# Experts' products of a transformer block in plain fp32 instead of three fp32r products, with a longer pipeline

## What is computed

```python
# 1. adapter with weights made from the condition
x0 = x + relu(x @ w_down(cond)) @ w_up(cond)
# 2. attention, causal, 16 query heads and 4 key/value heads of 64, RoPE, a sink in the denominator
x2 = x0 + attention(rmsnorm(x0, w1)) @ proj_w + proj_b
# 3. mixture of 32 experts, 4 per token
h2 = rmsnorm(x2, ffn_norm_w)
topv, topi = top_k(h2 @ gate_w + gate_b, 4);  gw = softmax(topv)
for n in range(32):                       # W_up[n]: 256 x 512, W_down[n]: 256 x 256
    ug = h2 @ W_up[n];  u, g = ug[:, :256], ug[:, 256:]
    y2 += combine[:, n] * ((silu(g) * u) @ W_down[n])
out = x + x2 + y2
```

## Time and profile before

| | |
|---|---|
| median of 3 runs | 1193.15 us (1192.16 to 1199.51) |
| the profiled execution: span | 1193.3 us |
| TensorE (PE) busy | 988.5 us, 83% |
| DVE busy | 766.5 us, 64% |
| POOL busy | 711.0 us, 60% |
| ACT busy | 451.5 us, 38% |
| read from HBM, written to HBM | 140.37 MB, 90.05 MB |
| first up product of stage two (L984) | 645.78 us |
| first sum of the tail (L1620) | 1161.07 us |

### The profile page before, as it was taken

The page is one execution under the profiler, slowest core; times in us unless marked ns, Lnnn a source line. Parts: engine busy times, 40 slices in busy tenths (PEclk is TensorE's granted clock), DMA queues, the critical chain, the costliest instruction groups (busy, mean ns, idle before and its releaser), DMA issues.

```text
span 1193.3 us, 19476 instructions
## 1 busy us (share of the span) xinstructions
PE 988.5 (83%) x6158; PEld 782.7 (66%) x6158; DVE 766.5 (64%) x1702; ACT 451.5 (38%) x1120; POOL 711.0 (60%) x672
## 2 busy tenths in 40 slices
PE   3779799999999998998834888888888888888896
PEld 1557576776767676676723776767767766676675
DVE  3868487776867777784672555555556555555568
ACT  1133243434343353424412444443444444444441
POOL 3426346858586776767485666666666666666550
PEclk8879899999999999998966999999999999999998
DMA  6328976565657756557566755574555546553498
GB/s 177 83 65 272 315 257 197 199 187 198 182 166 238 205 192 202 172 178 209 195 211 212 248 200 202 177 256 158 197 197 192 193 169 231 182 186 129 110 365 315
DMA packets 110749, 239.22 MB, mean 200 GB/s; under 512 B 19171, under 2 KB 48248, under 8 KB 109915
## 3 DMA queue, kind: packets, MB, share of 16 engines
q1 hardware_dynamic: 84042, 192.03, 48.5%
q0 software_dynamic: 19552, 40.02, 10.8%
q10 hardware_dynamic: 7056, 5.91, 1.6%
HBM read 140.37 MB, written 90.05 MB: 193 GB/s over the span
## 4 chain that ended last, share of the span: by engine, by line
PE 56%; DVE 19%; issue 9%; another core or an unknown queue 5%; ACT 4%; POOL 4%; DMA 2%; SPq 0%; ACTq 0%; DVEq 0%; POOLq 0%
PE gbank L984 16%; PE gbank L853 10%; PE gbank L1004 7%; PE gbank L778 4%; DVE ring L1339 4%; PE scores L814 4%; POOL lists L655 3%; ACT in_part L1194 2%; DVE in_part L1572 2%; PE gbank L756 2%; PE scores L995 2%; PE scores L957 2%; PE gbank L827 2%; PE gbank L748 1%
## 5 line engine op out<-in xcount | busy, mean ns | idle before, releaser
L984 PE MATMUL gbank<-ring,in_part 128*128 x954 | 271.4, 421 | 56.4 <-DVE in_part L1572 41.7
L700 POOL DMA_INDIRECT pick_rows<-rows_out,pair_row x156 | 161.0, 1032 | 150.9 <-ACT rows_out L1210 109.1
L984 PEld LDWEIGHTS gbank<-ring,in_part 128*128 128x128 f32 x954 | 173.3, 194 | 97.4 <-issue 67.8
L693 POOL DMA_INDIRECT rows_in<-x_rows,token_row x156 | 152.1, 975 | 55.4 <-issue 40.4
L1572 DVE SCALAR_TENSOR_TENSOR in_part<-scores,norm_w,in_part 128x128 fp32r<-128x128 f32 x318 | 96.3, 345 | 136.7 <-ACT in_part L1194 114.8
L1004 PE MATMUL gbank<-ring,mid_part 128*128 x954 | 155.7, 300 | 12.8 <-DVE mid_part L1593 9.3
L662 POOL TENSOR_TENSOR ring<-ring 128x512 fp32r<-128x512 f32 x96 | 121.0, 1279 | 72.1 <-ACT ring L1149 71.5
L655 POOL DMA_INDIRECT lists<-entry,slot_i x128 | 124.9, 976 | 38.8 <-issue 34.0
L853 PE MATMUL gbank<-w_o,ring 128*128 128x256 f32 x512 | 128.9, 409 | 17.1 <-DVE ring L1322 12.8
L1004 PEld LDWEIGHTS gbank<-ring,mid_part 128*128 128x128 f32 x954 | 126.6, 193 | 20.0 <-issue 19.9
L1210 ACT ACTIVATE rows_out<-gbank,gates 128x256 f32<-128x256 f32 x156 | 74.6, 478 | 154.5 <-PE gbank L1004 97.5
(11 more groups left out here) (169 smaller groups left out, 1495.3 us busy)
## 6 DMA issues: line engine op xcount, KB each, us to landing
w_parts<-ring SPq DMA_DIRECT2D x192, 256.0 KB
ring<-w_parts SPq DMA_DIRECT2D x32, 1536.0 KB
ring<-in_W_up SPq DMA_DIRECT2D x64, 256.0 KB
q_r<-rot SPq DMA_DIRECT2D x32, 512.0 KB, 6.1
picks<-pick_rows SPq DMA_DIRECT2D x8, 2048.0 KB
lists<-in_fill_slots SPq DMA_DIRECT2D x36, 256.0 KB, 5.0
ring<-in_W_down SPq DMA_DIRECT2D x32, 256.0 KB
x_t<-in_x_t SPq DMA_DIRECT2D x8, 512.0 KB, 5.0
```

What stands on the lines that cost most here:

```text
L693: e.indirect_dma_start(out=rows_in[i % NG][:, :], out_offset=None, in_=x2_rows, in_offset=bass.IndirectOffsetOnAxis(ap=begun[:, i, 3:4].bi ...
L700: e.indirect_dma_start(out=pick_rows, out_offset=bass.IndirectOffsetOnAxis(ap=begun_row[:, i:i + 1] if i < AHEAD else pair_row[:, i:i + 1] ...
L984: ins = e.matmul(bank[:, :], in_parts[i % 2][x][:, c, :], ring[:, bass.ds(at + y * WE + c * 2 * DFF, 2 * DFF)], start=k == 0, stop=k == le ...
```

## The change

The experts' products are computed in plain fp32: per tile 2 matmuls of 512 columns up and 2 of 256 down, on weights loaded from W_up and W_down as they lie, with two DMAs per expert (512 and 256 KB) straight into the ring. All load_third, split and store_third steps are gone from the lists of SP, ACT and POOL, and what is left of SP's list is spaced anew. The ring has 8 slots of one copy each; its last six lie over buffers of stage one (y_t, tmp, rot, prob_t), so experts 0 and 1 are loaded after SP's steps, 2 to 7 once stage one has let go of these. The turned rows (in_t) are one copy, the first half written by ACT, the second by DVE; the turned mid (mid_t) is one copy by DVE.

TensorE's order per tile becomes turn_mid(i-2), turn_in(i+2) with the wait for the expert's weights between its two transposes, expert_up(i), expert_down(i-3). turn_in and up share four PSUM banks, turn_mid and down four others. There are 3 buffers of in_t and mid, 8 of gathered rows (NG), 6 of rows_out (NY), and the scatter goes from i-2 to i-4. NET becomes 161, NPICK 5. The plan divides by 8 with a shift.

```diff
-NET = PAIRS // P + E - 1
-RING = 3
-AHEAD = RING
+AHEAD = 3
+NET = PAIRS // P + E - 1 + (AHEAD - 1)
+RING = 8
+FRONTS, BACKS = 4, 4
+IN_BUFS, MID_BUFS = 3, 3
-NW, NU, NPAY, NG, NY, NC = 5, 3, 3, 6, 4, 4
+NPAY, NG, NY, NC = 3, 8, 6, 4
-NPICK = 6
+NPICK = 5
...
     "POOL": ("""
         up pair pair pair pair pair up
     """, """
-        split split pair pair split split pair pair split split pair route_put split split split
-        route_put up route_put split split split route_put
+        pair pair pair pair pair route_put route_put up route_put route_put
     """, """
-        split split split split split route_put split split route_put split route_put split split split
-        route_put split route_put route_put route_put route_put
+        route_put route_put route_put route_put route_put route_put route_put route_put
...
         def load_expert(n):
             r = n % RING
-            e.dma_start(ring[:, r * 2 * WE:(r + 1) * 2 * WE].bitcast(F32).rearrange("p (h n) -> p h n", h=2),
-                        w_parts[n].rearrange("h p n -> p h n")).then_inc(s_weight[r], 16)
+            slot = ring[:, r * WE:(r + 1) * WE]
+            e.dma_start(slot[:, 0:KC * 2 * DFF].rearrange("p (c n) -> p c n", c=KC),
+                        d["W_up"][n].rearrange("(c p) n -> p c n", p=P)).then_inc(s_weight[r], 16)
+            e.dma_start(slot[:, KC * 2 * DFF:WE].rearrange("p (c n) -> p c n", c=FC),
+                        d["W_down"][n].rearrange("(c p) n -> p c n", p=P)).then_inc(s_weight[r], 16)
...
-        for i in range(NET + 2):
+        for i in range(NET + 4):
             if i + NG - 1 < NET:
                 gather(i + NG - 1)
-            if i >= 2:
-                scatter(i - 2)
+            if i >= 4:
+                scatter(i - 4)
...
+        def turn_in(i, ready=None):
+            bank = front[i % FRONTS]
             w.wait_ge(s_rows_in[i % NG], 16 * (i // NG + 1))
-            if i >= 2:
-                w.wait_ge(s_in_lower, i - 1)
+            if i >= FRONTS:
+                w.wait_ge(s_mid, i - FRONTS + 1)
             for c in range(KC):
+                if c == 1 and ready is not None:
+                    e.wait_ge(s_wready, ready)
                 ins = e.transpose(bank[:, c * P:(c + 1) * P], rows_in[i % NG][:, c * P:(c + 1) * P], ident[:, :])
...
-            for k, (c, x, y) in enumerate(CHUNK_PRODUCTS):
-                ins = e.matmul(bank[:, :], in_parts[i % 2][x][:, c, :],
-                               ring[:, bass.ds(at + y * WE + c * 2 * DFF, 2 * DFF)],
-                               start=k == 0, stop=k == len(CHUNK_PRODUCTS) - 1)
+            for c in range(KC):
+                ins = e.matmul(front[i % FRONTS], in_t[i % IN_BUFS][:, c, :], ring[:, bass.ds(at + c * 2 * DFF, 2 * DFF)],
+                               start=c == 0, stop=c == KC - 1)
             ins.then_inc(s_ug, 1)
...
         def expert_down(i):
-            out, at = gbank[2 + i % 2][:, 0:D], slot_of[i][0]
+            out, at = back[i % BACKS][:, D:2 * D], slot_of[i][0]
             w.wait_ge(s_mid_parts, i + 1)
-            if i >= 2:
-                w.wait_ge(s_rows_out, i - 1)
-            for k, (c, x, y) in enumerate(CHUNK_PRODUCTS):
-                ins = e.matmul(out, mid_parts[i % 2][x][:, c, :],
-                               ring[:, bass.ds(at + y * WE + KC * 2 * DFF + c * D, D)],
-                               start=k == 0, stop=k == len(CHUNK_PRODUCTS) - 1)
+            for c in range(FC):
+
+                if c == 1 and i + 2 >= BACKS:
+                    w.wait_ge(s_rows_out, i + 2 - BACKS + 1)
+                ins = e.matmul(out, mid_t[i % 2][:, c, :], ring[:, bass.ds(at + KC * 2 * DFF + c * D, D)],
+                               start=c == 0, stop=c == FC - 1)
             ins.then_inc(s_used, 1)
...
-        for i in range(NET + 2):
+        for i in range(NET + 3):
+            if i == 5:
+                w.wait_ge(s_gates, 2)
+            if 2 <= i < NET + 2:
+                turn_mid(i - 2)
             if i < NET:
+                ready = slot(i)[1]
+                if 0 < i < NET - 2:
+                    turn_in(i + 2, ready)
+                else:
+                    e.wait_ge(s_wready, ready)
                 expert_up(i)
...
-        def split(q):
-            w.wait_ge(s_whole[q % NW], 16 * (q // NW + 1))
-            if q >= NU:
-                w.wait_ge(s_lower, q - NU + 1)
-                w.wait_ge(s_upper_out[q % NU], 16 * (q // NU))
-            e.activation(w_upper[q % NU], w_third[q % NW].bitcast(F32), ACT.Copy).then_inc(s_upper, 1)
...
         def expert_down(i):
 
-            w.wait_ge(s_used, i + 2)
             if i >= NY:
                 w.wait_ge(s_put[i % NY], 16 * (i // NY))
+            w.wait_ge(s_used, i + 2)
```

More of the change, by code:

```diff
@@ L124 @@
     """, """
[L125 to L128 removed]
+        store_x2 store_x2 store_x2 store_x2
     """),
@@ L414, in program @@
              "slot_i"))
[L415 to L416 removed]
+    (s_list_tile, s_expert, s_gates, s_token_row, s_ring_wait, s_plan, s_in_whole, s_mid, s_mid_parts, s_final) = (
+        sem(f"s_{n}") for n in ("list_tile", "expert", "gates", "token_row", "ring_wait", "plan", "in_whole", "mid",
                                 "mid_parts", "final"))
@@ L1220, in scalar_program @@
         w.wait_ge(s_begun, 16)
-        for i in range(NET + 2):
+        for i in range(NET + 3):
+            if 0 < i < NET - 2:
+                turn_in(i + 2)
             if i < NET:
                 expert_up(i)
-            if i >= 2:
-                expert_down(i - 2)
-            if i + 2 < NET:
-                turn_in(i + 2)
+            if i == 0:
+                turn_in(2)
+            if i >= 3:
+                expert_down(i - 3)
             if i % XSTEP == 0 and 2 <= i // XSTEP < 2 + NT // NX:
@@ L1535, in vector_program @@
         e.tensor_scalar(of_tile[:, 3, :], of_tile[:, 0, :], float(E - 1), None, ALU.min).then_inc(s_expert, 1)
-        assert RING == 3 and all(43 * k >> 7 == k // RING for k in range(E))
+        assert RING == 8
         w.wait_ge(s_plan_row, 1)
-        got = own.mark(e.tensor_scalar(plan_e[:, :], plan_row, 43.0, None, ALU.mult))
+        got = own.mark(e.tensor_copy(plan_e[:, :], plan_row))
         w.wait_ge(s_vector, got)
-        got = own.mark(e.tensor_scalar(plan_e[:, :], plan_e[:, :], 7, None, ALU.arith_shift_right))
+        got = own.mark(e.tensor_scalar(plan_e[:, :], plan_e[:, :], 3, None, ALU.arith_shift_right))
         w.wait_ge(s_vector, got)
@@ L1604, in vector_program @@
         for i in range(NET + 2):
+            if i == 1:
+                slots()
+            if i >= 2:
+                turn_mid(i - 2)
+            if 0 < i < NET - 2:
+                turn_in(i + 2)
             if i < NET:
                 expert_mid(i)
-            if 1 <= i <= NET:
-                turn_mid(i - 1)
-            if i == 1:
-                slots()
-            if i + 2 < NET:
-                turn_in(i + 2)
+            if i == 0:
+                turn_in(2)
             if i % XSTEP == 0 and 3 <= i // XSTEP < 3 + NT // NX:
```

204 lines of the change are left out of this document (64 added, 140 removed).

## The result

The kernel after takes 1228.44 us (median of 4 runs, 1225.15 to 1230.91) beside 1194.08 for the kernel before: ratio 1.028, interval 1.026 to 1.031. Forecast were 1170 us (1145 to 1216). It is slower where it was forecast faster.

The account below looks back on a forecast made before the run. TensorE was taken to bound stage one, and TensorE and POOL neck and neck, with stalls, stage two. 1193.3 - 12.5 (stage two) - 4 (stage one) - 8 (transition) = 1168.8, forecast as 1170 us, range 1145 to 1216.

Parts of the forecast that it names:

- Products, tiles and stalls in stage two: Stage two: 161 fp32 tiles of 3.02 us, stalls nearly gone, 502.7 us against 515.2, so -12.5 us.
- the 8 us for left-over stalls: Stage two: 0.05 us of stall per tile left, 8 us in all; bounds nothing and today's 0.65 per tile.
- two readings of the stall: Stage two: rows_out's four slots wait for the scatter of i-4, or TensorE's signal comes late while POOL issues indirect DMAs.
- Rival A: Stage two: late signals still stall the ring of dependences; 1265 us with all stalls kept, 1213 with half; chance 0.15.
- Weights and tail: Stage two and tail: expert weights loaded early cost nothing; one pick buffer less costs 0, at worst +4 us.
- Splits out of stage one: Stage one: removing POOL's splits, ACT's copies and their loads and stores gives -4 us, bounds +10 and -30.
- the transition: Between stages: the last 32 puts, without 7 splits between them, end 8 us earlier; bounds -10 and -3.
- my 12: Stage one and transition together: -4 us for the splits and -8 us for earlier last puts.
- rival C: Whole kernel: no stalls, freer DVE and half of stage one's 36 idle us gone, 1148 us; chance 0.11.
- Rival B: Stage one: late signals beside runs of eight puts, 4 to 5 us in six periods, +24 to +30; 0.22 with partial stalls.
- 103 us of stalls removed: Stage two of the kernel before: some 103 us of waits, 0.65 per tile, of which the change would leave 8.
- The rule that I weighed: Stage one: VectorE and GpSimd share ports, first starter keeps them; removing 121 us of splits would then give more than 4 us.

Follow-up runs that it names:

- before_four_3: Kernel before with a fourth fp32r product per chunk in the up product, in a held session: 1205.36 us, ratio 1.010 to the kernel before.
- before_pipe: Kernel before, its fp32r products and split weights kept, with after's stage-two pipeline (order, banks, buffers, scatter i-4), held session: 1190.29 us, ratio 0.995.
- before_four: Kernel before with a fourth fp32r product per chunk in the up product, in a free session: 1154.39 us, ratio 1.051 to the kernel before.
- after_same_2: Kernel after, unchanged, run again in a free session: 1139.83 us, ratio 1.040 to the kernel before.
- after_wait4: Kernel after with POOL waiting behind each tile's four puts until they have landed: 1151.12 us in a free session, 5.1% slower than the kernel before.
- before_grouped: Kernel before, every split kept, POOL's steps reordered so puts stand in runs of eight, not four; free session: 1131.8 us, ratio 1.032.
- before_grouped_3: Kernel before with its puts in runs of eight, every split kept, in a held session: 1229.48 us, ratio 1.032 to the kernel before.
- after_wait4b: Kernel after with POOL waiting for each tile's four puts to land, in a held session: 1162.80 us, ratio 0.974 to the kernel before.
- after_dummy4: Kernel after with two scratch subtractions on POOL behind each tile's four puts, free session: 1152.78 us, 5.2% slower than the kernel before.

## Why the prediction was wrong

**Products, tiles and stalls in stage two: right.** 3.02 us per tile was forecast and measured. The stage was put at 502.7 and is 491.9; the 8 us for left-over stalls were not needed, and 2 or 3 us of the 8.5 for filling and draining neither. Of the two readings of the stall that I had left open, each has a part: slack alone takes it from 0.65 to 0.26 per tile (before_four_3), distances alone to 0.60 (before_pipe), both together, in the kernel after, to nothing. Rival A didn't come true: late signals are there, but TensorE's steps don't wait for them.

**Weights and tail: right, nearly.** There is no wait for weights in stage two. The tail is 2.6 us longer; I had 0, at worst 4.

**Splits out of stage one: the step that failed.** I put it at -4 us, with +10 as the bound for "new order of the puts", and the transition at -8. In a held session, as the forecast's own, the two came to +51. The runs show two terms of opposite sign. Without held signals the removal gains 32 us (645.6 to 613.3; the 645.6 is from a held session, but before_four, whose stage one is the same, has 643.8 and 640.0 in free ones and 643.9 in a held one, so 27 to 32), 15 to 20 more than my 12: the period falls from 68.4 to 65.9 us, 2.5 in each of seven groups, and the last put is issued at 598.26 in place of 632.34. What in the period gives the 2.5 us I haven't taken apart. I had let the last 32 puts begin at 584.65 as before; they begin at 559.11, since their slots come earlier. That is rival C's gain in stage one and more, though not by its reason. Held signals then cost 83 us.

**Rival B was the mechanism, mis-sized.** It had the runs of eight and the late signal, with 4 to 5 us in six periods and no doubt about the end: +24 to +30, where 83 were measured. The period is 78.5 us, against 65.9 for the same kernel in a free session. The chains of both, cut at the same steps, put the 12.5 us in four places:

- 5.4 are the late signal under the second run of the period. That is about B's size, and about that of the two waits behind the one run of eight in the kernel before (5.4 and 4.4 us).
- 3.0 are TensorE's scores (L768) beside the other run of eight: 5.06 us from 267.98 to the next step, with gaps that nothing ended, where the free session has 2.01.
- 2.6 are the product behind them (L710) at the lower clock: 5.42 us at 273.04, granted clock 0.50, where the earlier trace rows has 2.77.
- 1.5 are L807's sixteen passes right behind the late signal: 5.16 us at 220.98, granted clock 0.72, where the free session has 3.69.

So B's term was sized as a wait alone; what TensorE loses behind the wait and beside the run is more than the wait. Up to the first put of the last group (574.49 against 514.22) this makes 60 of the 83 us. The other 23 come from the end list of POOL. Stripped of its splits it puts sixteen puts in a row, twice: beside attention steps (574.49 to 594.41, the wait of 19.25 us) and beside the last routing steps (630.36 to 650.25, the wait of 14.14). I read that list as belonging to the transition, where TensorE is idle anyway.

**The sign of each term hangs on the session.** In held sessions the change costs 2.8% (1.028, in two sessions), in the one free session in which the kernel after ran unchanged 4.0% (1.040). I had not imagined the second kind. There the kernel before has hardly a stall to lose: its stage two takes 420.8 us, and 159 x 2.54 + 8.5 = 412.4. Then the change adds 69 us in stage two (489.7 against 420.8), takes 32 in front of it and adds 3 in the tail: 40, where the medians differ by 43. So the sum's largest gain, 103 us of stalls removed, was no property of the kernel alone. The trace of before couldn't show that; three runs within 0.6% of each other made it look like one. The time of the new stage two, forecast at 502.7, hardly depends on the session (491.9 held, 489.7 free); what depends on it is the stage that it replaces.

**The rule that I weighed.** DVE's cast that took 4.11 us beside three splits does so in all five held traces of the kernel before and its variants (4.11 to 4.12), where it starts 0.36 us ahead of the splits. In the five free ones it starts 1.2 us ahead and takes 0.17, and there other small DVE steps last as long as a split beside them (before_four: 1.53 us at 609.18, the split 609.40 to 610.67). I had said that the row agrees with the rule of the Trainium skill ("SBUF — State Buffer", section "SBUF: two separate sides"). It does in that both end together; it doesn't in that DVE had started first by the record, and by the rule should have kept the ports. The gain in stage one isn't explained by it: without any split the cast's longest is 0.253 us (after_same_2), but the large DVE instructions (L1359, 1232 ns mean) keep 1232.

**No kernel here is best in both kinds of session.** after_wait4 beats both in a held one (1163 against 1195 and 1229), the kernel before is best of those run in a free one (1097; before_pipe met none).

## What to carry to other kernels

Work that seems to hide in an idle engine may also be spacing something: before taking it out, write down what then stands back to back on that engine, above all runs of indirect DMAs on POOL, and what of TensorE runs beside them. Price a late signal up to the time left until the run would end, and add what the engine loses beside the run and behind the wait; here that was more than the wait (7.1 of 12.5 us per period). And a stall that no engine owns should be measured in more than one session before a change is built on its removal.

## What the hardware showed that I had not expected

The kernel before took 1193 to 1195 us in four sessions and 1097 in three, the two kinds met on one and the same chip, and within a session the runs of a kernel agree to about 1%. Neither the clock nor the pace of POOL accounts for the 9%: the kernel before was granted 0.93 to 0.94 in held sessions and 0.94 to 0.95 in free ones, and a scatter takes POOL 1031 ns in before_grouped and 1033 in before_grouped_3. Nearly all of the 97 us lie in stage two, in waits for signals of TensorE while POOL issues indirect DMAs. In held sessions a signal came up to 12.4 us late (kernel after, at 584.97); in free ones no list of waits, of twelve traces, has a line that ends on "remote". What makes a session one or the other stayed open; no kernel here could choose it. TensorE's own passes are spaced too under a long run (11 passes in 8.8 us, 3.5 of them gaps). So what is held may be TensorE as a whole rather than its signal; no run separates the two. The length of the run matters, but not alone: in held sessions sixteen gave 12.4 us, eight 0.03 to 5.5. Pauses behind every fourth put, in which POOL only waits some 1.4 us or more for its puts to land, let nearly all signals of stage one through (in after_wait4b one wait on a late signal is left, 4.8 us); whether two subtractions do as well in a held session wasn't measured, since after_dummy4 met a free one.
